# Five passes over 128 rows, three products per head instead of two, and ones in the tail: twelve sublayers in one launch on Trainium2

## The reference

```python
def _L2_ffn_ref(x, Wr, Wg, Wu, Wd, Wsg, Wsu, Wsd):        # F = 176, E = 8, K = 2
    shared_out = (silu(x @ Wsg.T) * (x @ Wsu.T)) @ Wsd.T
    scores = softmax(x @ Wr.T)
    topk_scores, topk_idx = top_k(scores, K)
    ...
    routed_out = sum over the two experts of score * ((silu(x @ Wg[e].T) * (x @ Wu[e].T)) @ Wd[e].T)
    return routed_out + shared_out

def _L2_attn_ref(x, Wq, bq, Wk, bk, Wv, bv, Wo, bo):      # H = 16, HD = 16
    scores = einsum("bhqd,bhkd->bhqk", q, k) / sqrt(HD)
    attn = softmax(where(causal, -inf, scores))
    ctx = einsum("bhqk,bhkd->bhqd", attn, v)
    return ctx.reshape(b, t, D) @ Wo.T + bo

def _L3_ffn_ref(x, weight, bias):
    return x @ ternary_quantize(weight).T + bias
```

## Time and profile before

| what | us |
|---|---|
| median of 3 runs | 1251.0 |
| lowest and highest run | 1250.42, 1256.68 |
| the profiled execution | 1242.25 |
| its span, first to last instruction | 1240.4 |
| TensorE busy | 1108.8 (89%) |
| VectorE busy | 853.0 (69%) |
| ScalarE busy | 617.6 (50%) |
| GpSimd busy | 543.9 (44%) |

### The profile page before, as it was taken

How to read it: one execution, slowest core, us unless ns; L and a number is a source line. 1 busy time by engine, 2 the same in 40 slices (tenths; PEclk the granted TensorE clock), 3 DMA queues, 4 the chain that set the end, 5 groups by cost and what they waited for, 6 DMA issues and landing times.

```text
span 1240.4 us, 21764 instructions
## 1 busy us (share of the span) xinstructions
PE 1108.8 (89%) x6538; PEld 918.7 (74%) x6538; DVE 853.0 (69%) x2406; ACT 617.6 (50%) x1440; POOL 543.9 (44%) x658
## 2 busy tenths in 40 slices
PE   5887688999899999987888899996799998999996
PEld 4776357777667878865666577885699997899995
DVE  4577766778978767758868866675766655665666
ACT  2455834321114345557748856554455553555552
POOL 5576718741445450235424417223354442544430
PEclk9898999999899999999899999997999998999998
DMA  5225322230013033422102163343011110010101
GB/s 174 65 65 192 112 79 77 86 106 20 1 42 144 9 107 104 128 65 56 38 16 50 40 229 108 115 121 101 26 43 34 40 36 26 26 52 25 51 0 34
DMA packets 48611, 88.12 MB, mean 71 GB/s; under 512 B 9680, under 2 KB 28496, under 8 KB 48080
## 3 DMA queue, kind: packets, MB, share of 16 engines
q1 hardware_dynamic: 42544, 75.41, 19.2%
q0 software_dynamic: 3968, 8.85, 2.4%
q10 hardware_dynamic: 2016, 2.83, 0.7%
HBM read 61.50 MB, written 19.27 MB: 65 GB/s over the span
## 4 chain that ended last, share of the span: by engine, by line
PE 52%; DVE 19%; ACT 6%; issue 4%; POOL 2%; DMA 1%; SPq 0%; DVEq 0%; POOLq 0%; ACTq 0%
PE ps L291 15%; PE ps L292 14%; PE ps L293 14%; DVE a_ptl L1908 4%; PE ps L1884 4%; DVE a_p L1845 2%; ACT a_p L1853 2%; DVE x L1607 1%; PE ps L877 1%; ACT a_pth L1900 1%; PE ps L909 1%; PE ps L427 1%; DVE stats L337 1%; DVE x L1060 1%; DMA raw<-moe_y,m_pos 1%
## 5 line engine op out<-in xcount | busy, mean ns | idle before, releaser
L1871 POOL TENSOR_SCALAR a_p<-a_p,small 128x128 f32<-128x128 f32 (+3 forms) x256 | 131.8, 532 | 224.0 <-DVE small L1862 223.8
L1853 ACT ACTIVATE a_p<-a_p,small 128x128 f32<-128x128 f32 (+3 forms) x256 | 141.6, 554 | 77.4 <-DVE small L1845 76.4
L1908 DVE TENSOR_TENSOR a_ptl<-ps,a_pth 128x384 fp32r<-128x384 f32 (+1 forms) x192 | 106.5, 595 | 56.7 <-ACT a_pth L1900 56.6
L291 PE MATMUL ps<-xh,wh 128*128 128x512 f32 x304 | 126.0, 414 | 10.2 <-POOL wl L526 5.8
L292 PE MATMUL ps<-xl,wh 128*128 128x512 f32 x304 | 122.4, 403 | 0.0
L293 PE MATMUL ps<-xh,wl 128*128 128x512 f32 x304 | 122.0, 401 | 0.0
L1900 ACT ACTIVATE a_pth<-ps 128x384 fp32r<-128x384 f32 (+1 forms) x192 | 90.3, 522 | 57.1 <-PE ps L1884 56.7
L1845 DVE CUSTOM_DVE_ANT_0 a_p<-ps,maskrow 128x128 f32<-128x128 f32 (+3 forms) x256 | 111.9, 483 | 4.5 <-PE ps L293 2.6
L403 POOL TENSOR_TENSOR rstd<-veps,nhalf 128x4 f32<-128x4 f32 x24 | 26.0, 1084 | 182.6 <-DVE veps L347 182.6
L1884 PE MATMUL ps<-ident,a_p 128*128 128x128 f32 x640 | 88.3, 287 | 7.9 <-DVE a_kl L1908 3.8
L495 POOL TENSOR_TENSOR wl<-raw,wh 128x256 fp32r<-128x256 f32 (+1 forms) x64 | 88.6, 1384 | 5.3
(11 more groups left out here) (393 smaller groups left out, 3412.2 us busy)
## 6 DMA issues: line engine op xcount, KB each, us to landing
raw<-in_w SPq DMA_DIRECT2D x32, 384.0 KB, 3.1
raw<-in_qk SPq DMA_DIRECT2D x16, 512.0 KB, 3.5
raw<-moe_x SPq DMA_DIRECT2D x60, 128.0 KB, 2.2
moe_y<-m_y SPq DMA_DIRECT2D x60, 128.0 KB, 1.7
m_raw<-in_ex SPq DMA_DIRECT2D x8, 608.0 KB, 7.5
m_a<-in_ex SPq DMA_DIRECT2D x8, 608.0 KB, 5.3
raw<-in_v SPq DMA_DIRECT2D x16, 256.0 KB, 2.6
moe_x<-drh SPq DMA_DIRECT2D x8, 480.0 KB, 5.8
```

The source lines that it names most:

```text
L291: pe.matmul(o, l[0], r[0], start=start, stop=False, skip_group_check=True)
L1853: s.activation(p[:, par, P_AT[i]:P_AT[i + 1]], p[:, par, P_AT[i]:P_AT[i + 1]], ACT.Exp, bias=h_nmx[:, par, i:i + 1], scale=scale, accum_ou ...
L1871: g.tensor_scalar(pp, pp, h_inv[:, par, i:i + 1], 1.0, ALU.mult, ALU.mult).then_inc(sem("at_norm"), 1)
L1908: ins = v.tensor_tensor(dst, ps[:, bank, 0:cols], f32(hi), ALU.subtract)
```

## The change

The fifth pass of `tile_down` takes all 128 rows of the tail instead of 64. In `att2` the groups are eight heads, high and low parts lie in two operands, a head's context is made by three passes instead of two, with one read-out in mid-unit (head 8) instead of three, and the output projection has two groups, 24 products per batch. The split of the value operand is four copies of 128 columns per group in place of one of 256. The transfer and the split of the second half of the output weights are dropped. GpSimd writes the zeros (six memsets of 1536 columns) behind its scatters. `dve_combine` comes one turn later (`late = 5`), the statistics in pairs at 9 and 10. `pe_warm` is called in the waits of the tail.

```diff
-                pe.matmul(o, tail[0:HF], m_b[0:HF, bass.ds(at + (2 * DC * FE + D), D)], start=False, stop=True,
+                pe.matmul(o, tail, m_b[:, bass.ds(at + (2 * DC * FE + D), D)], start=False, stop=True,
...
-                if m == 0 and 6 <= n - n0 < 12:
-                    k = n - n0 - 6
-                    v.memset(f32((drh, drl)[k % 2][:, (k // 2) * 1408:min((k // 2 + 1) * 1408, V_ZERO)]), 0.0)\
-                        .then_inc(sem("a2_vzero"), 1)
                 late = n - (n0 + NT)
-                if 4 <= late < 4 + TT:
-                    dve_combine(v, u, late - 4)
-                if 8 <= late < 8 + TT:
-                    dve_stats(v, u + 2, (late - 8,))
+                if 5 <= late < 5 + TT:
+                    dve_combine(v, u, late - 5)
+                if 9 <= late < 11:
+                    dve_stats(v, u + 2, (2 * late - 18, 2 * late - 17))
...
             if m == 0:
-                pool_wo2(g)
+                for k in range(6):
+                    g.memset(f32((drh, drl)[k % 2][:, (k // 2) * 1536:(k // 2 + 1) * 1536]), 0.0).then_inc(sem("a2_vzero"), 1)
...
             if u == 18:
+                pe_warm(pe, 8, 3)
+                pe.wait_ge(sem("x_res0"), 4 * 10)
+                pe_warm(pe, 13, 3)
                 pe_T(pe, 20)
+                pe_warm(pe, 6, 3)
             if u >= 22:
+                if u == 23:
+                    pe_warm(pe, 6, 3)
                 pe_ready(pe, u)
                 units_done(pe, u)
                 pe_scale3(pe, u)
+                if u == 22:
+                    pe_warm(pe, 8, 3)
                 pe_T(pe, u + 1)
...
-        def pe_transpose_p(pe, n, par, p, banks, earlier):
+        def pe_transpose_p(pe, n, par, p, banks, earlier, warm=0):
             pe.wait_ge(sem("at_norm"), TT + n * TT)
             for f, blocks in enumerate(FILLS):
+                if warm and f == 1:
+                    pe_warm(pe, warm, 7)
...
-                    pe.matmul(o, a2_v(kb, h), a2_pth[:, r], start=(h % VG_N == 0 and kb == 0), stop=False,
-                              skip_group_check=True)
-                    last = pe.matmul(o, a2_v(kb, h), a2_ptl[:, r], start=False, stop=(h % VG_N == VG_N - 1 and kb == TT - 1),
-                                     skip_group_check=True)
-                last.then_inc(sem("a2_pv"), 1)
+                if h % 8 == 0:
+                    pe.wait_ge(sem("a2_vlo"), TT * (2 * b + h // 8 + 1))
+                pe_pv(pe, ps[:, 6 + h // 8, :], f0 + 4 + 3 * h, lambda kb: a2_v(kb, h % 8), a2_pth, a2_ptl,
+                      h % 8 == 0, h % 8 == 7).then_inc(sem("a2_pv"), 1)
...
-            for t in range(2):
-                outp(t, range(VG - 1))
-            pe.wait_ge(sem("a2_zlo"), VG * (b + 1))
-            for t in range(2):
-                last = outp(t, (VG - 1,))
-            last.then_inc(sem("a2_out"), 1)
-            for t in range(2, TT):
-                last = outp(t, range(VG))
-            last.then_inc(sem("a2_out"), 1)
+            pe.wait_ge(sem("a2_zlo"), 2 * (b + 1))
+            for t in range(TT):
+                last = mm3c(pe, acc(t), [xTt(b, c, t) for c in range(DC)], [rc(1536 + c * D, D) for c in range(DC)])
+                if t % 2:
+                    last.then_inc(sem("a2_out"), 1)
...
-                s.activation(a2_vslot(g, 0), a2_vsrc(g), ACT.Copy).then_inc(sem("a2_vhi"), 1)
+                for t in range(TT):
+                    s.wait_ge(sem("a2_vf"), 4 * b + t + 1)
+                    s.activation(a2_vslot(True, t), a2_vf[:, t, g * P:(g + 1) * P].rearrange("p (h n) -> p h n", h=8),
+                                 ACT.Copy).then_inc(sem("a2_vhi"), 1)
...
-                if h == 1:
-                    v_hi(1)
-                if h in (5, 9, 13):
-                    act_z(s, b, (h - 5) // VG_N)
-                if h in (5, 9):
-                    v_hi((h - 5) // VG_N + 2)
+                if h == 8:
+                    act_z(s, b, 0)
+                    v_hi(1)
...
-            sp_wo2(sp)
```

More of the change, by code:

```diff
@@ L269, in build @@
             lin_qh=([P, DC, T], F32R), lin_ql=([P, DC, T], F32R))
+        VS = P + HD2
         (a2_qh, a2_ql, a2_kh, a2_kl, a2_vf, a2_sk, a2_pth, a2_ptl, a2_p) = sublayer_tensors(
@@ L1915, in pt_cols, with a2_v, a2_vslot @@
             return PT_AT[FILLS[f][0]], PT_AT[FILLS[f][-1] + 1]
[L1919 to L1947, removed]
-        def pool_wo2(g):
-            at = slice(WO_AT, WO_AT + 2 * D)
-            g.wait_ge(*since("a2_wo_in", 16))
-            g.tensor_scalar(drh[:, at], wo_raw[:, at], 1.0, 1.0, ALU.mult, ALU.mult).then_inc(sem("a2_wo_hi"), 1)
-            g.wait_ge(*since("a2_wo_hi", 1))
-            g.tensor_tensor(drl[:, at], wo_raw[:, at], f32(drh[:, at]), ALU.subtract).then_inc(sem("a2_wo_lo"), 1)
+        def a2_v(kb, j):
+            lo = slice(j * P, j * P + P)
+            return drh[:, kb * 8 * VS:(kb + 1) * 8 * VS][:, lo], drl[:, kb * 8 * VS:(kb + 1) * 8 * VS][:, lo]
+        def a2_vslot(hi, kb):
+            return (drh if hi else drl)[:, kb * 8 * VS:(kb + 1) * 8 * VS].rearrange("p (h n) -> p h n", h=8)[:, :, 0:HD2]
         def pe_att2(pe, u):
@@ L2013, in pe_att2 @@
             pe_T(pe, u + 1)
-            if b == 0:
-                pe.wait_ge(*since("a2_wo_lo", 1))
-            pe.wait_ge(sem("a2_zlo"), VG * b + VG - 1)
-            def outp(t, groups):
-                for g in groups:
-                    last = mm3(pe, acc(t), [z[:, t * P:(t + 1) * P] for z in a2_z(b, g)], a2_wo(g),
-                               g == 0 and t % 2 == 0, g == VG - 1)
-                return last
-            for t in range(2):
-                outp(t, range(VG - 1))
-            pe.wait_ge(sem("a2_zlo"), VG * (b + 1))
-            for t in range(2):
-                last = outp(t, (VG - 1,))
-            last.then_inc(sem("a2_out"), 1)
-            for t in range(2, TT):
-                last = outp(t, range(VG))
-            last.then_inc(sem("a2_out"), 1)
+            pe.wait_ge(sem("a2_zlo"), 2 * (b + 1))
[3 more added lines that the diff above has]
+                    last.then_inc(sem("a2_out"), 1)
         def act_att2(s, u):
@@ L2091, in v_lo @@
             def v_lo(g):
-                v.wait_ge(sem("a2_vhi"), VG * b + g + 1)
-                v.tensor_tensor(a2_vslot(g, 1), a2_vsrc(g), f32(a2_vslot(g, 0)), ALU.subtract).then_inc(sem("a2_vlo"), 1)
+                for t in range(TT):
+                    v.wait_ge(sem("a2_vhi"), TT * (2 * b + g) + t + 1)
+                    v.tensor_tensor(a2_vslot(False, t), a2_vf[:, t, g * P:(g + 1) * P].rearrange("p (h n) -> p h n", h=8),
+                                    f32(a2_vslot(True, t)), ALU.subtract).then_inc(sem("a2_vlo"), 1)
             v.wait_ge(sem("a2_vzero"), 6)
@@ L2124, in dve_att2 @@
                     dve_fill(v, f0 + 4 + 3 * h + f, f, a2_ptl[:, lo:hi], a2_pth[:, lo:hi], hi - lo)
-            dve_z(v, b, VG - 1)
+            dve_z(v, b, 1)
             dve_T(v, u + 1)
@@ L2262, in pair @@
                     pe_transpose_p(pe, n + hh, hh, a3_p, [bank["p", hh, f] for f in range(3)],
-                                   [starts["p", hh, f] for f in range(3)])
+                                   [starts["p", hh, f] for f in range(3)], 11 if side and first and hh == 0 else 0)
                     if side and first and hh == 1:
@@ L2960, in layout @@
     a["rope_feat"] = np.ascontiguousarray(tab.transpose(2, 0, 1))
-    wo = f["L2_attn_Wo"].T.reshape(VG, VG_N, 1, HD2, D)
-    wo = np.concatenate([wo, wo], axis=2).reshape(VG, P, D).transpose(1, 0, 2).reshape(P, VG * D)
-    a["att2"] = np.concatenate([rows_by_chunk(f["L2_attn_W" + k].T) for k in "qkv"] + [wo[:, 0:2 * D], sh[:, 2 * SLOT:]], axis=1)
-    a["att2_wo"] = wo[:, 2 * D:]
+    a["att2"] = np.concatenate([rows_by_chunk(f["L2_attn_W" + k].T) for k in "qkvo"] + [sh[:, 2 * SLOT:]], axis=1)
     a["att_cols"] = np.ascontiguousarray(np.concatenate([f["L2_attn_bq"].reshape(DC, P).T, f["L2_attn_bk"].reshape(DC, P).T], axis=1))
```

43 lines of the change are left out of this document (9 added, 34 removed).

## The result

The changed kernel takes 1240.15 us in the median of nine runs, against 1251.0 before: ratio 0.991 (95% interval 0.9885 to 0.9937), about 11 us less. Timed once more it came to 1234.14 us, ratio 0.988 (0.985 to 0.991). The forecast was 1229.7, 21.3 us less. So the direction and the range held, and a quarter to a half of the forecast gain is missing. The first timing lies outside the 1222 to 1237 us of the likeliest case and nearer to the first rival's 1242.9, so the time alone doesn't speak for the mechanism; the stages have to. The question of this part is where the missing gain went.

The account below looks back on a forecast made before the run. TensorE bounds the tile loops; attention 2's plain heads run on VectorE and ScalarE. Loops 15.7, attention 2 1.7 and ones 3.9 us sum to 21.3 us off the 1251.0 us median: 1229.7 us, range 1219 to 1243.

Parts of the forecast that it names:

- the likeliest case: Whole kernel: 21.3 us less, 1229.7 us, alone within 1222 to 1237 us; chance 0.60.
- the first rival: Fifth pass: the 64 rows are not the cause, tile stays 2.35 us, 8.1 us less, 1242.9 us; chance 0.12.
- The zeros: Tile loop: without VectorE's memset of 1.23 us before the next tile's work, 2.5 us come back.
- With 128 rows I expect two ordinary steps of 0.12: Fifth pass of each tile: 0.28 us less, a tile of 2.07 us, 16.8 us for 2 x 30 tiles.
- 1.1 us per loop for the turns with additions: Tile loops: VectorE's 2.62 us turns with additions outlast the new tile, so 1.1 us of gain per loop is given back.
- its other 0.7: Tile loops: row statistics in pairs and the last three tiles give back 0.7 us per loop.
- Attention 2: Heads 2.9 us more, read-outs 1.6 less, output projection 3.0 less: 1.7 us less in sum.
- TensorE becomes the bound: Attention 2: TensorE idles 0.44 us per head, 0.60 is added; all paid, 16.3 us lost again, 1246.0 us; chance 0.13.
- The one long head at the read-out: Attention 2, head 8: remaining read-out put at 1.5 us, twice the old; read-outs in all 1.6 us less.
- The output projection: After attention 2's heads: 24 products per batch instead of 48, 1.5 us less per batch, 3.0 us in all.
- the third pass: Attention 2: 0.60 us more per head, 0.24 paid in 12 plain heads, 2.9 us more; other heads cover it.
- The ones: Waits of the tail: products of ones keep TensorE's clock up, 3.9 us less, bounds 5.8 less and 1.3 more.

Follow-up runs that it names:

- table_moved: Changed kernel with TensorE's read of the next tile's weight offset from the table moved behind the gate and up products; ratio 0.984 to before.
- ones_only: Kernel before with only the products of ones in the tail added; 1243.47 us, ratio 0.996.
- two_pass: Changed kernel without the third pass of attention 2 (low part of the value operand left out); 1229.59 us, ratio 0.983 to before.
- weights_late: Changed kernel with VectorE's small products that make the routing weights at turn 9 of the loop instead of turn 4; ratio 0.987 to before.
- after_again: The changed kernel, unaltered, run and profiled once more; 1234.14 us, ratio 0.988 to before.

## Why the prediction was right, and where it was not

**Right in direction and mechanism.** The pause belonged to the 64 rows. The Trainium skill ("TensorE: Matmul & The Clock Gate", section "Why this matters for your kernels"), which spoke for the rival, says that a single product over few rows takes as long as one over 128. No run here has such a product alone; between others it cost more, and with 128 rows the steps around it fell from 0.21 and 0.31 us to 0.12 and 0.19. The zeros came back as forecast, the six memsets on GpSimd lie under its wait for the stores, and 31.42 us were left of that wait:

```profile
463.54 1.41 POOL L1267 MEMSET drh<- 128x1536 f32 x1
...
470.15 1.41 POOL L1267 MEMSET drl<- 128x1536 f32 x1
```

**The step that failed first: "With 128 rows I expect two ordinary steps of 0.12".** The second became 0.19, the tile 2.18 to 2.19 and not 2.07, so 60 tiles give 9.8 us instead of 16.8. Of the 0.11 us missing per tile, 0.07 are in that step and the rest is in the transposes and the gate product after it. The forecast had asked the right question (is it the read of the table?) and had a right row for the answer: at the loop's end, with no read behind it, the pause was 0.31 too. That row shows that the read is not needed for the pause. It does not show that the read is free: the two lay over each other, and by the numbers of table_moved the pause hid about 0.11 of the read's 0.16 us. After the change the step at the loop's end is 0.12 (533.32 to 533.44 us), inside the loop 0.19; moving the read made it 0.12 there as well.

**The give-back was mis-sized: 1.1 us per loop for the turns with additions.** Nine tiles from the first gathers on took 22.97 and 22.79 us before, 1.8 and 1.7 above nine plain ones. After, they take 24.37 and 24.40, 4.7 above nine tiles of 2.19 (4.1 and 5.2 in the second profile): 3 us are given back per loop by this pair, so many that these nine tiles are longer than before although a tile is shorter. But the profile of before was spared. In ones_only the nine tiles take 23.19 and 23.86 us, 2.1 and 2.7 above plain ones, and against these 2.3 us are given back per loop. The sum had 1.1 us, with one wait of 1.37 us in it, and for the row statistics a part of its other 0.7. What came is ScalarE's standstill during the gathers, which it had at nothing. That it belongs to the burst of gathers is shown (it goes with them, and goes away when they are spread); that it is neither the stores' landing nor the place in ScalarE's program is shown too. By what way GpSimd's gathers stop ScalarE stays open.

**A wait that no step of the forecast had:** the small VectorE operation under GpSimd's subtraction, 1.50 us in the first profile of the changed kernel and 1.89 in the second instead of 0.17, in the second loop alone. With the tile after it, this made three tiles take 7.51 and 7.96 us in the two profiles where three plain ones take 6.56: 1.2 us in the mean. It is no work of the change: ones_only has 0.6 us of it (7.65 us for three tiles of 2.35), and only the profile of before is without it.

In sum, in the loops: 9.8 + 2.5 - 6 - 1.2 = 5.1 us, against 5.25 by the first pair of profiles and 15.7 forecast. Against the loops of ones_only, which have the standstill and the collision too, the sum is 9.8 + 2.5 - 4.6 - 0.6 = 7.1 us, and the changed kernel's loops are 6.8 and 6.5 us shorter.

**Attention 2: 1.7 us less forecast, about nothing measured.** A head was put at 0.24 us more; it is 0.29 (4.49 against 4.20). Heads with row statistics didn't cover it: they went from 4.40 to 4.49, since the chain through TensorE now sets the pace of both. This is near the rival "TensorE becomes the bound" in its mechanism, at 0.29 us and not at 0.60 per head; TensorE itself still idles 0.21 us in a head (0.44 before). The one long head at the read-out is 5.76 us (692.88 to 698.64), where 4.20 + 1.5 was forecast. The output projection is as forecast: 731.30 to 734.22 us, 2.9 instead of 5.80, and from the last head's transposes to the next unit's second set of transposes 21.2 us instead of 22.7, 1.5 less. The price of the third pass is read from two_pass: the second batch's heads take 66.00 us from the first transposes to the last, and 69.2 with the third pass. That is 3.2 us, where the sum had 8 x 0.24 = 1.9 for this batch. In the first batch, where heads also add gathered rows and executions differ more, the changed kernel's profiles are 4.7 and 2.2 us longer than two_pass's, and those of table_moved and weights_late 0.9 and 1.0, where the sum had 1.0.

**The ones: 3.9 forecast, 4.5 measured (1.9 to 7.1).** By the first pair of traces the stretch from the last fifth product to the end of the twelve products is 3.1 us shorter (forecast 2.2), from there to the next unit's transposes 1.0 (0.9), and the end 1.6 (0.8). The clock did not fall in the 1.49 us that the ones left open. The forecast had 2.4 us open, by 21 products of 0.21 us; half of its 0.45 is 0.225, which gives 4.7 us (4.71 measured) and leaves 1.9 of the 6.64.

So the likeliest case was the right one by its shorter tile, the zeros, the output projection and the clock, with its largest term put at 16.8 us instead of 9.8 and the give-back of the gathering turns at 1.1 us per loop instead of 2.3 to 3. That the first timing lies within the range is in part luck: the range's upper end was drawn for a rival that did not come.

## What to carry to other kernels

A pause that is removed uncovers what lay under it: ask of everything else in the gap how long it would be alone, since a row where it is absent shows only that the pause doesn't need it. A loop made shorter runs against whatever doesn't get shorter with it (here the turns with gathers and additions), so price those turns on the new beat, one by one. And a profile is one execution: where its own time is 0.7% from the median, as here, look at the same code in other kernels' profiles before its rows carry a term, and before a wait that is only in the new profile is put down to the change.

## What the runs showed of the hardware that was not expected

While GpSimd issues four gathers back to back, ScalarE stands still for 1 to 2.6 us ahead of operations whose inputs are long there (2.53 us in turn 19 of the changed kernel); with one gather per tile it does not (below 0.7 us). By what way is not shown.

TensorE's read of a register from a table costs it 0.16 to 0.17 us per tile between the fifth product and the next tile's gate products (0.67 us against 0.51 for that stretch, 0.07 of it in the first step), and about 0.11 us behind the gate and up products.

A VectorE operation of 0.17 us took 1.39 to 1.89 us when a GpSimd subtraction of 2.38 us had started before it (ones_only and the two profiles of the changed kernel), and 0.17 us when it started 0.09 us ahead of one (before).

The granted clock falls in other places from one execution to the next, on the same code. A stretch far ahead of the change, windows of after and then of before:

```profile
170.00:173.00 3.00, 3.00 (x14) 2.53 (x14) 1.19 (x5) 1.43 (x3) 1.25 (x2) 0.50 0.00 0
```

```profile
170.00:173.00 3.00, 3.00 (x19) 1.79 (x18) 1.49 (x6) 1.42 (x3) 1.25 (x2) 1.00 0.00 0
```

TensorE was busy throughout in both, and got through 14 products in the one, 19 in the other. In after_again, the same kernel as after, the clock was 1.00 in that window. By such stretches, and by waits of 1.5 to 2 us that come and go, the first fifth product lies at 462.76 us in the profile of before and between 464.42 and 470.94 in the others, with nearly the same instructions ahead of it. That is more than half of what this change is worth, and the reason why its parts had to be read from stages and not from spans.
